# Attention stage of a fused layer stack: order of the second half's values, the output row and the key loads

## The chip, the cores and the metric

The kernel runs on one core of a Trainium2 chip. A core has five engines that run their own instruction streams and wait for each other by semaphores: TensorE (PE, matrix products; its weight loads are shown as PEld), VectorE (DVE), ScalarE (ACT), GpSimd (POOL) and SyncE (SP, here used only to start transfers). The metric is the device time of one launch in microseconds (us), lower being better. The kernel before is shown with three timed runs and one profiled execution.

## What is computed

A stack of six layers on a residual x of 4096 rows (2 sequences of 2048, read by the attention as 4 of 1024) by 256 columns: half a gated feed-forward, gated delta attention, half a feed-forward, half a binary-weight layer, a state-space convolution, half a binary-weight layer. The change lies in the attention. Its core, per head (16 heads of 16 columns) and chunk of 64 rows:

```
P = where(strict, (k_beta @ k.T) * L, 0)        # L = exp(g_i - g_j), lower triangle
Ainv = (I + P)(I + P^2)(I + P^4)...             # the inverse of a triangular matrix
v = Ainv @ v;  k_cumdecay = Ainv @ (k_beta * exp(g))
def step(S, inp):                               # scan over the chunks
    attn  = where(tril, (q @ k.T) * L, 0)
    v_new = v - k_cumdecay @ S
    o     = (q * exp(g)) @ S + attn @ v_new
    S     = S * exp(g_last) + (k * exp(g_last - g)).T @ v_new
o = o * rsqrt(mean(o*o) + 1e-5) * norm_w * silu(gate)
x = x + o @ Wo
```

## The kernel before, in words

The stages run one after another with a barrier between them (`phase_end`): first feed-forward, gates (which computes the decays and writes the normalized, turned x to a scratch in DRAM), delta (the attention), feed-forward, binary, space, binary. The delta stage works on 32 tiles of 128 rows (each in two halves of chunk length 64) with a software pipeline: `SLOTS` = 40 slots, and in slot n each engine runs a fixed list of steps, written out by hand, for tiles of different ages. `at(step, t)` runs a step for tile t if there is such a tile. LAG_FORM is 1, LAG_PAD 5, LAG_APPLY 6, LAG_SCAN 7 (the tile Z = n - 7 whose state is advanced) and LAG_OUT 8 (the tile O = n - 8 whose output row is finished).

PE, in slot n: values and states of the first half (`from_values` L1431, `from_state` L1450), `project_qk` (L1360) of tile n, `to_state` (L1463), the turned q and k and the decays of tile n - 1 (L1390, L1378, L1381), the second half's values and states, `project_vg` (L1370), `to_state` of the second half, `turn_o` (L1495) of O, `apply` (L1416, the product with the inverse T), `outputs` (L1481, L1486) of Z, `within` (L1400) of n - 1 and `project_o` (L1501) of O. The gate of tile n and `outputs` of tile Z are tied by a wait: `outputs` waits for the semaphore p_gate of tile n.

ACT: the copies y of the values (`keep_y`, L1615, halves 0 and 1), `widen` (L1631), the squares of q and k (L1530), `keep_kq` (the copies MV L1574 and KT L1575, the latter releasing the semaphore f_kt), `root_qk`, `exp_decays`, the value and gate copies and the sigmoid (L1557 to L1559), copies of the transposed output, WT, UT, the pad, and of the output (`keep_o`); `root_o` (L1549, L1550) is the reciprocal root of the output's mean square.

DVE interleaves two kinds of work: the triangular solve of a pair of tiles, in 58 steps of mostly one instruction each (L1750 to L1764; 29 in a slot, the first half in slots with even n), and small ones: `own_heads` (L1771, L1779), `new_state`, `sum_qk`, `faded_q` (QgT, L1704, which waits for f_kt), `keep_gate` (L1688), `scale_qk` (QK, L1696), `keep_within` and `keep_attn` (PT, AT, L1713), `sum_o` (L1790), `scale_o` (L1795), `add_o` (L1799).

POOL: the state's fades and sum (L1871, L1878, L1883), `gate_o` (L1887), `decayed_k` (L1854) and `kept_k` (L1864), which need QK. SP: all transfers of the stage, in the order of its slots: the turned x of tile n + 1, the decays, the keys out to DRAM (tile n - 1) and in again in another layout (`keys_in`, L1305, four transfers, tile n - 2), PT out and, by pairs of tiles, the matrices of the solve in and out. All transfers wait in SP's single order.

Of the kernel before, what the change touches and what calls it, by code (L numbers as in the profile page):

```python
# [12 lines left out]
P = 128  # L13
# [56 lines left out]
def build(nc, io):  # L70
    ctx = ExitStack()
    with ctx:
# [94 lines left out]
        late.close()  # L167
        B.gates_xn, B.ffn_xn, B.binary_xn = made["gates"].xn, made["ffn"].xn, made["binary"].xn
# [801 lines left out]
def gates_sync(e, B, M, S, run):  # L970
# [295 lines left out]

def delta_sync(e, B, M, S, run):
    Pd, Td = B.P_dram, B.T_dram

    def turned_in(t):  # L1270
        if t >= 2:
            e.wait_ge(S.p_vg, t - 1)
        b = t // BLK
        e.wait_ge(S.xt_out[b % 2], 32 * (b // 2 + 1))
        src = bass.AP(tensor=B.xT_dram, offset=t * P, ap=[[NT * P, P], [P * NT * P, KD], [1, P]])
        e.dma_start(M.xT[t % 2].rearrange("p (k n) -> p k n", k=KD), src).then_inc(S.p_in[t % 2], 16)
# [17 lines left out]

    def keys_in(t):

        e.wait_ge(S.k_out[t % 2], 16 * (t // 2 + 1))
        if t >= 2:
            e.wait_ge(S.k_in[t % 2], 64 * (t // 2))
        if t >= 7:  # L1300
            e.wait_ge(S.s_b, 2 * (t - 6))
        for r in range(4):
            src = bass.AP(tensor=B.Kd_dram, offset=t * P * DM + 8192 * r, ap=[[SUB, SUB], [1024, 8], [1, SUB]])
            dst = M.Kd[t % 7][SUB * r:SUB * r + SUB, :].rearrange("p (n c) -> p n c", n=8)
            e.dma_start(dst, src).then_inc(S.k_in[t % 2], 16)  # L1305
# [217 lines left out]
def delta_scalar(a, own, B, M, S, run):  # L1523
# [126 lines left out]
    for n in range(SLOTS):  # L1650
        Z = n - LAG_SCAN
        at(keep_y, Z, 0)
        at(root_o, n - LAG_OUT)
        at(widen, Z, 0)
        at(squares, n)
        at(keep_kq, n - LAG_FORM)
        at(root_qk, n)
        at(exp_decays, n - LAG_FORM)
        at(keep_y, Z, 1)
# [7 lines left out]
        at(keep_o, Z)  # L1667
    a.wait_ge(S.f_rstd, NBLK + 1)
# [5 lines left out]
def delta_vector(v, own, B, M, S, run):  # L1674
# [130 lines left out]
    for n in range(SLOTS):  # L1805
        Z, O = n - LAG_SCAN, n - LAG_OUT
        at(scale_o, O)
# [20 lines left out]
        solve(n, 24, 26)  # L1828
# [5 lines left out]
        at(sum_o, Z)  # L1834


def delta_gpsimd(g, own, B, M, S, run):
# [28 lines left out]

    def fade_first(t):
# [21 lines left out]
    for n in range(SLOTS):  # L1889
        Z, O = n - LAG_SCAN, n - LAG_OUT  # L1890
# [282 lines left out]
```

## Time and profile before

| | |
|---|---|
| runs shown | 1250.27, 1255.26, 1258.14 us (median 1255.26) |
| profiled execution | 1255.64 us, span 1253.8 us |
| granted PE clock, mean | 0.93 |
| PE / DVE / ACT / POOL busy | 1038.9 / 911.5 / 595.3 / 405.2 us |
| instructions | 38504 |
| delta stage | 224 to 844 us of the span |

A line of a timeline gives the start in us, the time that the instruction or group took, the engine, the line of the kernel, the operation with output and inputs, the number of instructions, and in brackets how long the engine had been idle ahead of it and which engine's work ended that. In a window the numbers behind the engines are busy us, in parentheses the instructions; behind them the granted clock of PE (1.00 is full speed), the share of the transfer engines and GB/s. The stage ends when x is complete, and the next one begins behind a barrier, so what the stage saves or loses the kernel saves or loses.

### The profile page before, as it was taken

How to read it: one execution, taken by the hardware profiler on the slowest of the kernel's cores; microseconds unless marked ns; L12 is line 12 of the kernel's file. 1: busy time of each engine (PE TensorE's matmuls, PEld its weight loads, DVE VectorE, ACT ScalarE, POOL GpSimd, SP SyncE). 2: the span in 40 equal slices, each digit the busy share in tenths (PEclk: the TensorE clock that was granted, in tenths of full speed). 3: DMA queues.
4: the chain of work that ended last, by engine and by line, in shares of the span. 5: the costliest groups of instructions: out<-in, count | busy, mean ns of one | idle time of the engine just before them, and what ended most of it. 6: DMA issues, size and time to landing. Idle time of an engine off the chain costs nothing. (4 is left out here: it accounts for less than half of the span.)

```text
span 1253.8 us, 38504 instructions
## 1 busy us (share of the span) xinstructions
PE 1038.9 (83%) x15542; PEld 738.8 (59%) x15542; DVE 911.5 (73%) x2403; ACT 595.3 (47%) x1614; POOL 405.2 (32%) x580
## 2 busy tenths in 40 slices
PE   2999977676888888888888876669999798799978
PEld 2888854344555555555555554548888664255556
DVE  3877646268888888988888888527776435899953
ACT  2433245344676666766767764454333352201152
POOL 2666530311221212122212221115665347500055
PEclk9999988798989999999999987779999889899979
DMA  9000012254444444444444443100000023944012
GB/s 259 8 2 1 1 56 101 61 103 95 105 96 95 92 91 91 105 101 96 83 97 99 100 93 75 36 3 1 1 1 1 17 57 79 268 135 135 1 34 101
DMA packets 282624, 93.30 MB, mean 74 GB/s; under 512 B 208976, under 2 KB 275408, under 8 KB 282448
## 3 DMA queue, kind: packets, MB, share of 16 engines
q1 hardware_dynamic: 280848, 88.23, 30.0%
q10 hardware_dynamic: 1600, 2.62, 0.7%
q8 instruction: 123, 2.02, 0.7%
q14 instruction: 53, 0.43, 0.1%
HBM read 56.20 MB, written 30.41 MB: 69 GB/s over the span
## 5 line engine op out<-in xcount | busy, mean ns | idle before, releaser
L1764 DVE TENSOR_TENSOR delta_tmp<-delta_PR 128x130 f32<-128x130 f32 (+12 forms) x416 | 156.5, 376 | 9.1
L1761 DVE TENSOR_TENSOR delta_PR<-delta_PR,delta_tmp 128x130 f32<-128x130 f32 (+12 forms) x416 | 152.7, 367 | 9.4
L1615 ACT ACTIVATE delta_y<-psum 32x128 f32<-32x128 f32 x256 | 68.1, 266 | 82.9 <-PE psum L1450 80.7
L1854 POOL TENSOR_TENSOR delta_VK<-delta_QK,both_eg 128x256 f32<-128x256 f32 x32 | 20.9, 653 | 253.7 <-DVE delta_QK L1696 253.7
L1416 PE MATMUL psum<-delta_T,delta_pad 128*32 128x128 f32 x2048 | 81.5, 326 | 17.5 <-DMA delta_T<-inverse_scratch 17.4
L1416 PEld LDWEIGHTS psum<-delta_T,delta_pad 128*32 128x32 f32 x2048 | 69.5, 133 | 28.3 <-DMA delta_T<-inverse_scratch 22.4
L1360 PE MATMUL psum<-both_w_in,delta_xT 128*128 128x512 f32 x128 | 68.0, 656 | 20.2 <-DMA delta_xT<-turned_scratch 10.2
L1878 POOL TENSOR_TENSOR delta_S<-delta_E,delta_Bm 128x128 f32<-128x128 f32 x32 | 16.4, 514 | 205.2 <-issue 198.2
L1463 PEld LDWEIGHTS psum<-delta_y,delta_Kd 32*32 32x32 f32 x2048 | 23.3, 112 | 99.3 <-ACT delta_y L1615 99.3
L506 POOL TENSOR_TENSOR ffn_H<-ffn_hid,ffn_H 128x512 fp32r<-128x512 f32 x48 | 61.7, 1290 | 57.2 <-DVE ffn_H L472 57.2
L1631 ACT ACTIVATE delta_wide<-delta_S 32x128 f32<-32x128 f32 x256 | 78.1, 305 | 3.1
L506 POOL TENSOR_TENSOR first_H<-first_hid,first_H 128x512 fp32r<-128x512 f32 x48 | 61.6, 1289 | 53.7 <-DVE first_H L472 53.7
L1463 PE MATMUL psum<-delta_y,delta_Kd 32*32 32x32 f32 x2048 | 30.6, 199 | 56.9 <-ACT delta_y L1615 56.9
L438 ACT ACTIVATE first_silu<-psum 128x512 f32<-128x512 f32 x48 | 28.7, 598 | 83.9 <-PE psum L391 83.9
L640 PE MATMUL psum<-w_bin,binary_XT 128*128 128x256 f32 x256 | 66.9, 407 | 0.0
L438 ACT ACTIVATE ffn_silu<-psum 128x512 f32<-128x512 f32 x48 | 28.7, 599 | 79.9 <-PE psum L391 79.9
L1370 PE MATMUL psum<-both_w_in,delta_xT 128*128 128x512 f32 x128 | 66.5, 645 | 0.0
L1400 PE MATMUL psum<-delta_MV,delta_KT 32*32 32x128 f32 x2048 | 63.9, 273 | 3.1 <-ACT delta_E L1565 3.1
L311 DVE BATCH_NORM_STATS2 ln_stats<-X 128x6 f32<-128x256 f32 x128 | 54.0, 422 | 16.6 <-DMA X<-in_x 14.4
L1400 PEld LDWEIGHTS psum<-delta_MV,delta_KT 32*32 32x32 f32 x2048 | 55.0, 107 | 12.8 <-issue 6.3
L709 DVE TENSOR_SCALAR binary_Y<-psum 128x512 f32<-128x512 f32 x32 | 22.1, 692 | 53.7 <-PE psum L640 53.7
L391 PE MATMUL psum<-first_XT,w_gate 128*128 128x512 f32 x192 | 54.6, 407 | 3.6 <-DVE first_XT L460 3.6
(282 smaller groups left out, 2599.0 us busy)
## 6 DMA issues: line engine op xcount, KB each, us to landing
within_scratch<-delta_PT SPq DMA_DIRECT2D x128, 64.0 KB, 1.9
delta_PR<-within_scratch SPq DMA_DIRECT2D x16, 512.0 KB, 4.3
inverse_scratch<-delta_PR SPq DMA_DIRECT2D x16, 512.0 KB, 3.3
delta_T<-inverse_scratch SPq DMA_DIRECT2D x128, 64.0 KB, 2.8
space_T<-taps_scratch SPq DMA_DIRECT2D x8, 1024.0 KB, 5.8
X<-taps_scratch SPq DMA_DIRECT2D x8, 1024.0 KB, 8.9
X<-in_x SPq DMA_DIRECT2D x32, 128.0 KB, 9.8
turned_scratch<-gates_XT SPq DMA_DIRECT2D x16, 256.0 KB, 2.3
```

The lines of the kernel that those rows point to most:

```text
L391: i = pe.matmul(bank[:], w[:, k * HID + m * P:k * HID + (m + 1) * P].bitcast(F32R), M.XT[b % 2][hl][k].bitcast(F32R), start=(k == 0 and hl ...
L438: a.activation(M.silu[n % 3], B.bank[n % 2][:], ACT.Silu, scale=1.0 / 127.0).then_inc(S.silu, 1)
L506: g.tensor_tensor(lo.bitcast(F32R), M.hid[n % 3], hi, ALU.subtract).then_inc(S.hid_lo, 1)
L640: i = pe.matmul(o[:, j * DM:(j + 1) * DM], M.XT[b % 3][k][:, (2 * h + j) * P:(2 * h + j + 1) * P], B.w_bin[:, k * DM:(k + 1) * DM], start= ...
L1360: i = pe.matmul(bank[4][:], M.xT[t % 2][:, k * P:(k + 1) * P], M.w_in[:, k, 0:512], start=(k == 0), stop=(k == 1))
L1370: i = pe.matmul(bank[5][:], M.xT[t % 2][:, k * P:(k + 1) * P], M.w_in[:, k, 512:1024], start=(k == 0), stop=(k == 1))
L1400: mm = pe.matmul(kk[g][rows, q * P:(q + 1) * P], M.KT[rows, g * P + SUB * q:g * P + SUB * q + SUB], M.MV[rows, (4 * g + q) * P:(4 * g + q ...
L1416: i = pe.matmul(bank[3][SUB * c:SUB * c + SUB, (2 * w + g) * P:(2 * w + g + 1) * P], M.pad[:, from_c:from_c + SUB], M.T[t % 2][:, h * P:(h ...
L1615: i = a.activation(dst, heads(bank[6][rows, half * P:(half + 1) * P]), ACT.Copy)
L1631: i = a.activation(states(M.wide[half])[rows, :, SUB * c:SUB * c + SUB], states(X)[rows, :, :], ACT.Copy)
L1761: i = v.tensor_tensor(after, after, t3, ALU.add)
L1764: i = v.tensor_tensor(t3, column.to_broadcast([P, j, n_after]), row.to_broadcast([P, j, n_after]), ALU.mult)
```

## The change

Five things. (1) The turned x of tiles 0 and 1 is loaded at the end of the gates stage (`turned_in` becomes a function that both stages call; the buffers xT of the delta stage are handed to the gates stage), instead of at the start of the delta stage. (2) On ACT the copy y of the second half's values stands ahead of the copies MV and KT. (3) The output row of a tile is finished in the slot of its scan: `sum_o`, `root_o`, `scale_o` and `gate_o` run in slot Z + 7 and no longer partly in the next. (4) On DVE QK stands ahead of the gate, and the gate four solve steps after `new_state` of the second half instead of three. (5) The loads `keys_in` are issued by POOL's queue, between the second fade and `decayed_k`, instead of SP's.

```diff
@@ gates_sync
+    for t in range(2):
+        turned_in(e, B, M.xT, S, t)
     taps_store(e, B, M, S)
@@ delta_sync
-    for n in range(-1, SLOTS):
-        at(turned_in, n + 1)
+    for n in range(SLOTS):
+        at(rows_in, n + 1)
         at(decays_in, n)
         at(keys_out, n - 1)
-        at(keys_in, n - 2)
@@ delta_scalar
         at(keep_y, Z, 0)
-        at(root_o, n - LAG_OUT)
         at(widen, Z, 0)
         at(squares, n)
+        at(keep_y, Z, 1)
         at(keep_kq, n - LAG_FORM)
         at(root_qk, n)
         at(exp_decays, n - LAG_FORM)
-        at(keep_y, Z, 1)
         at(widen, Z, 1)
...
         at(keep_o, Z)
+        at(root_o, Z)
@@ delta_vector
-        at(scale_o, O)
...
         at(new_state, Z, 1)
-        solve(n, 15, 18)
+        solve(n, 15, 16)
+        at(scale_qk, n)
+        solve(n, 16, 19)
         at(keep_gate, n)
-        solve(n, 18, 20)
-        at(scale_qk, n)
-        solve(n, 20, 23)
+        solve(n, 19, 22)
+        at(sum_o, Z)
+        solve(n, 22, 23)
         at(keep_within, n - LAG_FORM)
         solve(n, 23, 24)
         at(keep_attn, n - LAG_FORM)
-        solve(n, 24, 26)
+        solve(n, 24, 25)
+        at(scale_o, Z)
+        solve(n, 25, 26)
         at(add_o, O)
...
-        at(sum_o, Z)
@@ delta_gpsimd
+    def keys_in(t):
+        g.wait_ge(S.k_out[t % 2], 16 * (t // 2 + 1))
+        if t >= 2:
+            g.wait_ge(S.k_in[t % 2], 64 * (t // 2))
+        if t >= 7:
+            g.wait_ge(S.s_b, 2 * (t - 6))
+        for r in range(4):
+            ...
+            g.dma_start(dst, src).then_inc(S.k_in[t % 2], 16)
...
         at(fade_second, Z)
-        at(gate_o, O)
+        at(keys_in, n - 2)
         at(decayed_k, n)
         at(kept_k, n)
+        at(gate_o, Z)
```

On ACT, in a slot of the full stretch, the rows before, from the squares to the second `widen` (delta_y is the copy of the values, delta_KT the copy that f_kt announces):

```order
L1530 ACTIVATE delta_sq<-psum 128x512 [waits p_sum,p_qk]
L1574 ACTIVATE delta_MV<-psum,consts 128x2x8x32 [waits f_kk,f_kq_ps]
L1574 ACTIVATE delta_MV<-psum,consts 128x2x8x32
L1575 ACTIVATE delta_KT<-psum 128x256
L1542 ACTIVATE delta_rs<-delta_ssq,consts 128x32 [waits p_kn,p_sum]
L1543 ACTIVATE delta_rs<-delta_rs 128x32 [waits act_own]
L1565 ACTIVATE delta_E<-psum 128x512 [waits f_at,f_d]
L1615 ACTIVATE delta_y<-psum 32x8x16 [waits s_o,s_ws]
L1615 ACTIVATE delta_y<-psum 32x8x16 x3
L1631 ACTIVATE delta_wide<-delta_S 32x4x32 [waits s_o,s_1]
```

And now:

```order
L1525 ACTIVATE delta_sq<-psum 128x512 [waits p_sum,p_qk]
L1610 ACTIVATE delta_y<-psum 32x8x16 [waits s_o,s_ws]
L1610 ACTIVATE delta_y<-psum 32x8x16 x3
L1569 ACTIVATE delta_MV<-psum,consts 128x2x8x32 [waits f_kk,f_kq_ps]
L1569 ACTIVATE delta_MV<-psum,consts 128x2x8x32
L1570 ACTIVATE delta_KT<-psum 128x256
L1537 ACTIVATE delta_rs<-delta_ssq,consts 128x32 [waits p_kn,p_sum]
L1538 ACTIVATE delta_rs<-delta_rs 128x32 [waits act_own]
L1560 ACTIVATE delta_E<-psum 128x512 [waits f_at,f_d]
L1626 ACTIVATE delta_wide<-delta_S 32x4x32 [waits s_o,s_1]
```

The second half's delta_y has moved past MV, KT, the roots and the decays.

On DVE, the stretch from the state of the second half to PT (delta_tmp and delta_PR are the solve's), before:

```order
L1784 TENSOR_TENSOR delta_S<-delta_E,delta_Bm 128x128 [waits s_wide,s_e1,s_bm]
L1764 TENSOR_TENSOR delta_tmp<-delta_PR 128x198 [waits i_step]
L1761 TENSOR_TENSOR delta_PR<-delta_PR,delta_tmp 128x9x22 [waits i_step]
L1764 TENSOR_TENSOR delta_tmp<-delta_PR 128x210 [waits i_step]
L1688 TENSOR_TENSOR delta_gate<-delta_gate,psum 128x256 [waits p_sig,p_v]
L1761 TENSOR_TENSOR delta_PR<-delta_PR,delta_tmp 128x10x21 [waits i_step]
L1764 TENSOR_TENSOR delta_tmp<-delta_PR 128x220 [waits i_step]
L1696 TENSOR_TENSOR delta_QK<-psum,delta_rs 128x512 [waits p_kd,p_kg,f_kq_ps,p_rs]
L1761 TENSOR_TENSOR delta_PR<-delta_PR,delta_tmp 128x11x20 [waits i_step]
L1764 TENSOR_TENSOR delta_tmp<-delta_PR 128x228 [waits i_step]
L1761 TENSOR_TENSOR delta_PR<-delta_PR,delta_tmp 128x12x19 [waits i_step]
L1713 TENSOR_TENSOR delta_PT<-psum,delta_E 128x256 [waits i_out0,f_kk]
```

And now:

```order
L1779 TENSOR_TENSOR delta_S<-delta_E,delta_Bm 128x128 [waits s_wide,s_e1,s_bm]
L1759 TENSOR_TENSOR delta_tmp<-delta_PR 128x198 [waits i_step]
L1691 TENSOR_TENSOR delta_QK<-psum,delta_rs 128x512 [waits p_kd,p_kg,f_kq_ps,p_rs]
L1756 TENSOR_TENSOR delta_PR<-delta_PR,delta_tmp 128x9x22 [waits i_step]
L1759 TENSOR_TENSOR delta_tmp<-delta_PR 128x210 [waits i_step]
L1756 TENSOR_TENSOR delta_PR<-delta_PR,delta_tmp 128x10x21 [waits i_step]
L1683 TENSOR_TENSOR delta_gate<-delta_gate,psum 128x256 [waits p_sig,p_v]
L1759 TENSOR_TENSOR delta_tmp<-delta_PR 128x220 [waits i_step]
L1756 TENSOR_TENSOR delta_PR<-delta_PR,delta_tmp 128x11x20 [waits i_step]
L1759 TENSOR_TENSOR delta_tmp<-delta_PR 128x228 [waits i_step]
L1785 TENSOR_REDUCE delta_o_ss<-delta_o_sq 128x16 [waits o_rs,o_sq]
L1756 TENSOR_TENSOR delta_PR<-delta_PR,delta_tmp 128x12x19 [waits i_step]
L1708 TENSOR_TENSOR delta_PT<-psum,delta_E 128x256 [waits i_out0,f_kk]
```

QK has moved ahead of the gate and past four solve instructions, the gate is one solve instruction later, and `sum_o` (delta_o_ss) now stands ahead of PT.

On POOL, a slot, now (L1874 is `keys_in`; L1896 is `gate_o`, which stood behind the second fade before):

```order
L1880 TENSOR_TENSOR delta_E<-delta_S,both_egl 128x128 [waits s_x]
L1887 TENSOR_TENSOR delta_S<-delta_E,delta_Bm 128x128 [waits s_wide,s_bm,s_e0]
L1892 TENSOR_TENSOR delta_E<-delta_S,both_egl 128x128 [waits s_1]
L1874 DMA delta_Kd<-key_scratch 32x8x32 [waits s_b,k_in0,k_out0]
L1874 DMA delta_Kd<-key_scratch 32x8x32 x3
L1851 TENSOR_TENSOR delta_VK<-delta_QK,both_eg 128x16x16 [waits u_pad,p_kn]
L1861 TENSOR_TENSOR delta_Kd_tok<-delta_QK,both_bekd 128x4x32 [waits k_out0,p_kn]
L1861 TENSOR_TENSOR delta_Kd_tok<-delta_QK,both_bekd 128x4x32
L1896 TENSOR_TENSOR delta_o_sb<-delta_o_sb,delta_gate 128x256 [waits o_mul]
```

The four issues stand behind the second fade and ahead of `decayed_k` (delta_VK).

## Rows read from the trace of the kernel before

**Rows 1.** Windows of the whole core; engines' busy us (instructions), granted clock, DMA share.

```profile
308.20:740.40 432.20, 366.11 (x9735) 244.75 (x9727) 380.24 (x1136) 294.20 (x947) 93.70 (x174) 0.96 0.45 95
```

**Rows 2.** Windows of the twelve slots with even n; sum in the last line.

```profile
604.32:620.04 15.72, 14.02 (x391) 9.30 (x390) 13.90 (x46) 11.71 (x38) 3.81 (x7) 1.00 0.47 105
...
sum 196.36, PE 171.16 PEld 115.39 DVE 171.06 ACT 140.96 POOL 45.65; mean PE 14.26 PEld 9.62 DVE 14.25 ACT 11.75 POOL 3.80
```

**Rows 3.** Windows of the last five of these, 570.70 on: their sum.

```profile
sum 78.91, PE 69.71 PEld 46.59 DVE 69.50 ACT 58.67 POOL 19.07; mean PE 13.94 PEld 9.32 DVE 13.90 ACT 11.73 POOL 3.81
```

**Rows 4.** Windows: the slot n = 25, and two microseconds within it.

```profile
620.04:638.23 18.19, 15.52 (x390) 10.57 (x389) 16.00 (x46) 11.82 (x38) 3.76 (x7) 0.91 0.47 91
...
630.00:632.00 2.00, 1.78 (x50) 1.34 (x54) 1.86 (x7) 1.92 (x7) 0.00 (x0) 0.62 0.45 108
```

**Rows 5.** Timeline of PE, slots n = 24, 25: start, us, group, [idle before <-releaser].

```profile
609.21 0.48 PE L1450 MATMUL psum<-delta_X,delta_WT 32*32 32x32 f32 x32
...
616.08 0.65 PE L1481 MATMUL psum<-delta_y,delta_AT 128*32 128x64 f32 x32
...
630.22 0.52 PE L1463 MATMUL psum<-delta_y,delta_Kd 32*32 32x32 f32 x32 [2.00 <-ACT delta_y L1615]
...
631.28 3.20 PE L1416 MATMUL psum<-delta_T,delta_pad 128*32 128x128 f32 x64
634.31 0.62 PE L1481 MATMUL psum<-delta_y,delta_AT 128*32 128x64 f32 x32
```

**Rows 6.** Timeline of ACT, slots n = 24 and 25.

```profile
608.53 0.60 ACT L1530 ACTIVATE delta_sq<-psum 128x512 f32<-128x512 f32 x1
...
610.31 0.38 ACT L1575 ACTIVATE delta_KT<-psum 128x256 f32<-128x256 f32 x1
...
611.54 1.09 ACT L1615 ACTIVATE delta_y<-psum 32x128 f32<-32x128 f32 x4
...
615.08 0.42 ACT L1559 ACTIVATE delta_gate<-delta_gate 128x256 f32<-128x256 f32 x1
...
627.00 0.38 ACT L1575 ACTIVATE delta_KT<-psum 128x256 f32<-128x256 f32 x1
```

**Rows 7.** Timeline of DVE, slots n = 24 and 25.

```profile
607.39 0.43 DVE L1795 TENSOR_TENSOR delta_o_sb<-delta_o_sb,delta_o_rs 128x256 f32<-128x256 f32 x1 [0.62 <-ACT delta_o_rs L1550]
...
611.37 0.42 DVE L1704 TENSOR_TENSOR delta_QgT<-psum,delta_egT 128x256 f32<-128x256 f32 x1
...
615.60 0.42 DVE L1688 TENSOR_TENSOR delta_gate<-delta_gate,psum 128x256 f32<-128x256 f32 x1 [0.37 <-ACT delta_gate L1559]
...
626.67 0.81 DVE L1764 TENSOR_TENSOR delta_tmp<-delta_PR 128x234 f32<-128x234 f32 x1
...
629.59 0.42 DVE L1704 TENSOR_TENSOR delta_QgT<-psum,delta_egT 128x256 f32<-128x256 f32 x1
...
633.50 0.41 DVE L1688 TENSOR_TENSOR delta_gate<-delta_gate,psum 128x256 f32<-128x256 f32 x1
```

**Rows 8.** Timeline of POOL, slot n = 24.

```profile
617.41 0.69 POOL L1854 TENSOR_TENSOR delta_VK<-delta_QK,both_eg 128x256 f32<-128x256 f32 x1 [7.10 <-DVE delta_QK L1696]
```

**Rows 9.** Timelines of POOL, PE, ACT, DVE where the stage starts.

```profile
224.05 0.20 POOL L1839 MEMSET delta_S<- 128x128 f32 x1 [45.54 <-DVEq L171]
...
229.73 3.75 PE L1360 MATMUL psum<-both_w_in,delta_xT 128*128 128x512 f32 x4 [7.82 <-DMA delta_xT<-turned_scratch]
...
238.64 3.75 PE L1360 MATMUL psum<-both_w_in,delta_xT 128*128 128x512 f32 x4 [2.86 <-DVE delta_QK L1696]
...
235.28 0.23 ACT L1543 ACTIVATE delta_rs<-delta_rs 128x32 f32<-128x32 f32 x1
...
237.81 0.68 DVE L1696 TENSOR_TENSOR delta_QK<-psum,delta_rs 128x512 f32<-128x512 f32 x1
```

**Rows 10.** One line's DMA issues on SP: duration ns min/median/max.

```profile
L1305 SPq DMA_DIRECT2D delta_Kd<-key_scratch x128: 303/463/2098, 255.2 to 766.5; - x128
```

**Rows 11.** Timeline of PE, the stage's last slot.

```profile
840.91 0.44 PE L1495 MATMUL psum<-consts,delta_o_sb 128*128 128x128 f32 x2 [2.69 <-POOL delta_o_sb L1887]
```

More of the change, by code:

```diff
@@ L167, in build @@
         late.close()
+        made["gates"].xT = made["delta"].xT
         B.gates_xn, B.ffn_xn, B.binary_xn = made["gates"].xn, made["ffn"].xn, made["binary"].xn
@@ L1264, in at, with turned_in, rows_in @@
         stage(t, *more)
+def turned_in(e, B, xT, S, t):
+    b = t // BLK
+    e.wait_ge(S.xt_out[b % 2], 32 * (b // 2 + 1))
+    src = bass.AP(tensor=B.xT_dram, offset=t * P, ap=[[NT * P, P], [P * NT * P, KD], [1, P]])
+    e.dma_start(xT[t % 2].rearrange("p (k n) -> p k n", k=KD), src).then_inc(S.p_in[t % 2], 16)
 def delta_sync(e, B, M, S, run):
     Pd, Td = B.P_dram, B.T_dram
-    def turned_in(t):
+    def rows_in(t):
         if t >= 2:
             e.wait_ge(S.p_vg, t - 1)
[L1273 to L1276, printed above, removed]
+            turned_in(e, B, M.xT, S, t)
     def decays_in(t):
@@ L1293, in keys_out @@
         e.dma_start(dst, M.Kd_tok[t % 2].rearrange("p (n c) -> p n c", n=8)).then_inc(S.k_out[t % 2], 16)
[L1295 to L1305, printed above, removed]
     def pair_in(m):
@@ L1865, in kept_k @@
         i.then_inc(S.p_kd, 1)
+    def keys_in(t):
[5 more added lines that the diff above has]
+        for r in range(4):
+            src = bass.AP(tensor=B.Kd_dram, offset=t * P * DM + 8192 * r, ap=[[SUB, SUB], [1024, 8], [1, SUB]])
+            dst = M.Kd[t % 7][SUB * r:SUB * r + SUB, :].rearrange("p (n c) -> p n c", n=8)
+            g.dma_start(dst, src).then_inc(S.k_in[t % 2], 16)
     def fade_first(t):
@@ L1889, in delta_gpsimd @@
     for n in range(SLOTS):
-        Z, O = n - LAG_SCAN, n - LAG_OUT
+        Z = n - LAG_SCAN
         at(fade_first, Z)
```

## Prediction

> **What bounds the kernel now.** I read the windows first (what a full slot takes, and how busy each engine is), then the timelines of single slots (what the engine that ends last was waiting for), then those of the stage's two ends. The attention stage runs in 40 slots, and 25 of them, full ones, take 432.2 us of the span [rows 1], 17.29 us each. In them PE is busy 366 us and DVE 380; no engine is full, so the slot is a chain that goes from engine to engine. A slot with n even takes 16.36 us in the mean (twelve of them, 196.36) [rows 2], so one with n odd takes 235.8/13 = 18.1; the slot n = 25 is such a one, 18.19 [rows 4].
>
> The pair n = 24, 25 shows the chain. PE's slot n = 24 runs from 604.32 to 620.04 [rows 2]. DVE multiplies the gate at 615.60, and PE's `outputs` starts 0.48 us later, at 616.08; from there `outputs`, `within` and `project_o` run without a gap to the next slot at 620.04, 3.96 us [rows 5, 7]. So what ends last is the gate on DVE (`outputs` of one tile shares its turn with the gate of another), and a slot moves as the gate moves. In n = 24 the gate itself waited 0.37 us for the sigmoid on ACT, whose last step runs from 615.08 [rows 6, 7]: there two chains, DVE's and ACT's, end nearly together. In n = 25 DVE's gate stands at 633.50 without a wait, but the product with T ahead of `outputs` took 3.20 us at a granted clock of 0.62 (between the full 2.4 GHz and the lower level, 1.2), after PE had stood idle 2.00 us for the keys' half y [rows 4, 5]; `outputs` went at 634.31.
>
> **Part 1, the early rows.** Before, the stage opens at 224.05 (POOL's first instruction behind the barrier) and PE's first projection at 229.73, held by the load of the turned x [rows 9]. The load of tiles 0 and 1 now is issued in the stage before, behind the stores of the turned rows. The first projection can start right behind the barrier, at 224.1: 5.6 us. Then QK of tile 0: its scale was ready at 235.51, but it stood behind the gate and ran at 237.81, and PE waited 2.86 us for it [rows 9]. QK now goes ahead of the gate: 2.2 us. In slots 1 and 2 QK stands behind the gate too, and would give about 1 us each, as PE's own work there is next. The sum is 9.6 us (5.6 + 2.2 + 1.8) until the first triangular solve starts. It can't be over 12 (7.8 of wait at PE, 2.9 at QK, 1 more); it can be as little as 0 if the fill is bound by the loads of the decays, whose issues on SP stand where they stood. The nearest rows are those of PE, which waits for the rows and for QK and not for the decays, so I take 9.6.
>
> **Part 2, the slots with n even.** ACT now does the second half of y right behind the squares, ahead of the copies MV and KT. It needs `from_state` of the second half on PE, which starts at 609.21, behind PE's own row of work with no wait [rows 5]. `from_state` takes 0.48 [rows 5], so y can start at 609.73. ACT lost 0.6 us of work and a wait (root_o) ahead of the squares, which end at 609.13 now and at about 608.1 then [rows 6]. So ACT stands idle 1.6 us, y takes 1.09, MV 1.16, and KT starts at 612.0 instead of 610.31 and ends at 612.38. DVE's QgT waits for KT. It ran at 611.37, and DVE now comes to it 0.7 to 1.0 us earlier, since the wait of 0.62 for root_o is gone [rows 7]. So DVE stands 1.7 to 2.0 us and QgT runs at 612.40, 1.03 later than before. From QgT to the gate DVE had 4.23 us, of them 0.37 wait [rows 7]: 3.86. QK (0.68 by its row [rows 9], 0.60 net of its overlap with the next) and one more solve step (0.40, the length that a step has beside no POOL work) now lie ahead of the gate: 4.86. The gate stands at 617.26, 1.66 us later than 615.60, and the slot is 1.6 us longer. That holds for the last five even slots (78.9 us in all, 15.8 each) [rows 3]. The seven earlier ones take (196.36 - 78.9)/7 = 16.8, and the same chain gives about 17.3 there, +0.5. Sum: 5 x 1.6 + 7 x 0.5 = **+11.5**. Bounds: if QgT's wait didn't come, the gate would be bound by ACT, whose sigmoid chain is as long as before save for root_o, and the slot would be 16.3, no change (0). If every even slot paid 1.66, +19.9.
>
> **Part 3, the slots with n odd.** Here KT ended at 627.38 and DVE came to QgT at 629.59 [rows 6, 7], 2.2 us later; with y first KT ends at about 628.0, still half a microsecond or more ahead of DVE: no new wait. Gone are the wait of 0.62 and about 0.7 of sum_o and scale_o, which now run in the stretch behind the gate; QK and a step, 0.93, come ahead of the gate. The gate moves by -0.3 to 0 and the sum over 13 slots is -4 to 0. What PE gains at y (its 2.00 us of idle end earlier) turns into a wait for the gate, so I take **-0.6**.
>
> **Part 4, the tail.** In the last eight slots there is little solve left and the chain is root_o, scale_o, gate_o, turn_o, project_o. With sum_o, root_o, scale_o and gate_o done in the tile's own slot, the last row ends earlier: in the last slot PE waits 2.69 for gate_o on POOL [rows 11], and about 1.9 of that goes. Against it, in four slots in which the last solves run, scale_o and sum_o stand ahead of the result that is stored back: 0.35 + 1.3 + 1.0 (n = 32, 34, 35). I take **-0.2**, from -4 to +3.
>
> **Part 5, keys on GpSimd's queue.** SP issues 4 a tile at 0.46 us each, 2.1 at the most [rows 10], 1.9 us a slot that SP gets back; it only waits for PT with it: 0. On POOL they stand between the second fade (done about 5 us into the slot) and decayed_k, which waits 7.10 us for QK [rows 8]. POOL works 3.8 us a slot [rows 2]. By the rows four issues take 1.2 to 8.4 us; at 1.85 they fit in the 7.1, and only over 1.8 each would they be late. No row shows an issue from POOL. DVE's solve steps take 0.81 instead of 0.40 where a POOL instruction runs beside them (626.67) [rows 7]; if an issue did the same it would cost 0.4 a slot and issue. I take 0 and keep the rest as a rival.
>
> The Trainium skill, "SBUF — State Buffer", section "SBUF: two separate sides", speaks against this part: descriptors of a transfer that GpSimd's queue issues are written by GpSimd's cores, which are locked out of the port while DVE runs certain operations, and its next section gives about 620 ns alone and about 3100 ns beside a copy. By it, an estimate, four issues would take up to 12.4 us, and with POOL's own 3.8 the slot would be near its bound. No row of this trace shows such an issue.
>
> **The sum.** -9.6 + 11.5 - 0.6 - 0.2 + 0 = +1.1. To that comes PE's clock. PE will now stand idle ahead of `outputs` (for the gate) rather than ahead of y, 2 us and more, and in the slot n = 25 such a pause was followed by work at 0.62 [rows 4]. If it falls on `outputs` and `within` (3.2 us of work) and not on the product with T, it lies on the path; I put 1 to 2 us on it in the likeliest case. The profiled execution is 1255.64, by 0.4 above the median shown, so the forecast is 1255.6 + 2.4 = **1258**. Its own range is 1248 to 1268.
>
> **Rivals.**
> Faster, 0.24: QgT's wait stays hidden (y is not late in the even slots, or DVE's slack takes it up). Then part 2 is 0 and part 3 up to -4: 1255.6 - 9.6 - 2 = 1244. For it: ACT's and DVE's chains end within 0.4 us of each other [rows 7], and a shift of 0.5 us in either tips it. Against: the row of `from_state`, which has no wait to lose.
> Slower by the clock, 0.13: in the odd slots PE's pause ahead of `outputs` costs 0.9 to 2.1 us each, say 1.3 (3.2 us of work at 0.6 instead of 1.0 takes 2.1 longer, less the 3.20 x 0.38 = 1.2 that the product with T no longer loses, or all of it where that also stays slow). It decides once the pause is as long as the 2.00 of n = 25. Ten slots: 1258 + 13 = 1271.
> Slower by the issue on POOL, 0.18: from 1.8 us an issue, decayed_k and kept_k come late, with them the pad and the fades; or the issues slow DVE's solve steps, 4 x 0.4 = 1.6 us a slot, half of it on the path. At 0.6 to 0.8 us in 32 slots: +19 to +26, so 1277 to 1284. For it: 626.67. Against: the 7 us of room.
> The early load brings nothing (it queues behind the stores of the gates, or the decays bound the fill), 0.05: 1267.
> The forecast has 0.40.
>
> **How the numbers follow.** About 1% (12.5 us) is what a measurement of this kernel can tell from no change. Faster by it (below 1242.7) is about half of the first rival and the lower end of the forecast, with the tail: 0.20. Slower by it (above 1267.8): nearly all of clock and POOL, half of the lost load, the upper end of the forecast: 0.34. Within: 0.46. The range 1240 to 1278 leaves out a tenth at either end.
>
> **What would show it.** Right: PE's first projection at 224.1; on DVE a wait at QgT for KT of 1.7 us in the slots with n even alone, and even slots of 17.3; root_o's wait on DVE gone; odd slots within 0.3 of 18.1. Wrong: even slots of 16.3 or less; POOL's issues over 1.8 us or solve steps of 0.8 beside them; a granted clock under 0.7 at `outputs`. The sum fails most easily in part 2, as its +11.5 hangs on one wait.

## The result, and the profile after

The changed kernel takes 1277.42 us (median of 4, 1277.30 to 1284.25) where the kernel before took 1254.11 (4 runs): 1.0199 times as long, 95% interval 1.0152 to 1.0246. The forecast was 1258, 2.4 us more and no change that a measurement could tell; measured are 23.3 us more, clear of the interval. The time lies inside the stated range (1240 to 1278) by 0.6 us, but the size was missed. The profiled execution took 1284.25 us, 6.8 more than the median of the four, and spans 1282.5 us instead of 1253.8, so the differences by stage below are those of one execution each and add up to more than the 23.3 us. One of the ten runs of a later kernel, e7, took 1381.27 us at a granted clock of 0.73, a slower state, and is left out of its numbers.

Where the 28.7 us are, stage by stage, from the two traces: the first solve starts at 251.5 instead of 266.8 (-15.3, forecast -9.6); the 25 full slots take 467.2 instead of 432.2 (+35.0, forecast +10.9); the tail from there to the last product takes 110.2 instead of 102.6 (+7.6, forecast -0.2); the rest (+1.4) lies mostly in later stages. Of the start's 15.3 us, 1.6 are there because the stage before ended sooner (222.41 instead of 224.05).

The windows of the changed kernel, as [rows 1 and 2] had them; the last line of each group is the sum over its windows. First the 25 slots, then the twelve with n even, then the thirteen with n odd:

```profile
sum 467.18, PE 378.79 PEld 258.82 DVE 379.44 ACT 296.25 POOL 153.25; mean PE 378.79 PEld 258.82 DVE 379.44 ACT 296.25 POOL 153.25
```

```profile
sum 219.61, PE 180.67 PEld 124.53 DVE 173.07 ACT 142.47 POOL 72.91; mean PE 15.06 PEld 10.38 DVE 14.42 ACT 11.87 POOL 6.08
```

```profile
sum 247.57, PE 198.11 PEld 134.29 DVE 206.38 ACT 153.78 POOL 80.35; mean PE 15.24 PEld 10.33 DVE 15.88 ACT 11.83 POOL 6.18
```

DVE's work is the same (379 us); PE is 12.7 us busier with the same products, because it ran more of them at a low clock (granted clock 0.92 instead of 0.96 [rows 1]). Slots with n even went from 196.4 to 219.6, slots with n odd from 235.8 to 247.6.

What PE waited for in these 25 slots (engine and line, releaser: total, times, longest), in the kernel before and then in the changed one:

```profile
PE psum L1463 <- ACT delta_y L1615: 38.8, 25, 2.0
PE psum L1481 <- DVE delta_gate L1688: 10.5, 13, 1.0
PE psum L1431 <- DVE delta_Bm L1771: 6.8, 13, 0.8
PE psum L1416 <- DMA delta_T<-inverse_scratch: 5.3, 9, 1.1
PE psum L1450 <- DVE delta_X L1779: 4.2, 13, 0.3
```

```profile
PE psum L1411 <- DMA delta_T<-inverse_scratch: 59.4, 25, 4.2
PE psum L1476 <- DVE delta_gate L1683: 26.9, 15, 3.2
PE psum L1445 <- DVE delta_X L1774: 1.9, 6, 0.3
```

The wait for y is gone, and those for T and the gate grew from 15.8 to 86.3 us. PE's waits grew from 66 to 88 us, and they moved: from in front of `to_state` to in front of the product with T and of `outputs`. DVE's waits at sum_o and at QgT, 300 to 780 us:

```profile
DVE delta_o_ss L1785 <- ACT delta_o_sq L1633: 33.6, 26, 3.2
...
DVE delta_QgT L1699 <- ACT delta_KT L1570: 18.2, 13, 1.6
```

The slot n = 24 of the changed kernel, from 610.33, on DVE and on PE (start, us, group, idle before and its releaser):

```profile
618.45 0.42 DVE L1699 TENSOR_TENSOR delta_QgT<-psum,delta_egT 128x256 f32<-128x256 f32 x1 [1.60 <-ACT delta_KT L1570]
...
623.51 0.41 DVE L1683 TENSOR_TENSOR delta_gate<-delta_gate,psum 128x256 f32<-128x256 f32 x1
```

```profile
621.39 3.42 PE L1411 MATMUL psum<-delta_T,delta_pad 128*32 128x128 f32 x64 [3.02 <-DMA delta_T<-inverse_scratch]
624.57 0.88 PE L1476 MATMUL psum<-delta_y,delta_AT 128*32 128x64 f32 x32
```

The forecast wait at QgT is there, 1.60 us (forecast 1.7 to 2.0), and the gate stands at 13.18 us into the slot (forecast 12.94; 11.28 before [rows 7]). But `outputs` starts at 14.24 and not at 13.66, 0.48 behind the gate: PE had stood 3.02 us for T, and the product with T then took 3.42 us. That is the second thing. The forecast had half of it, the low clock behind a pause of PE, as a rival for the odd slots; that PE would stand for T stands nowhere in it.

The start, as [rows 9] (timelines of PE and DVE):

```profile
222.41 3.62 PE L1355 MATMUL psum<-both_w_in,delta_xT 128*128 128x512 f32 x4 [2.14 <-DVEq L172]
...
228.94 1.95 PE L1355 MATMUL psum<-both_w_in,delta_xT 128*128 128x512 f32 x4 [1.19 <-DVE delta_QK L1691]
```

```profile
251.52 0.09 DVE L1737 MEMSET delta_PR<- 128x32 f32 x1
```

PE waits for the stage's barrier and no longer for the load. The second projection ran 3.75 us at the low clock before and runs 1.95 now, so 1.8 of the extra 5.7 us of gain is clock. The pause right ahead of it shrank from 2.86 to 1.19 us, but it isn't that pause alone: in e5 below it is 3.04 us, and the projection takes 1.95 as well. What e5 and the changed kernel both lack is the 7.82 us of idle time ahead of the first projection.

The key loads on GpSimd's queue:

```profile
L1874 POOL DMA_DIRECT2D delta_Kd<-key_scratch x128: 582/582/798, 235.5 to 785.7; - x128
```

Each issue takes 0.58 us, 2.3 a slot, within the 7 us of room [rows 8]. The DVE steps beside them kept their length (0.26 to 0.29 us for the steps of 108 and 130 columns, as in the kernel before).

### The profile page after: what moved, and what is told of

The parts are those of the page before. It is cut to its first block and busy times, and to the rows that moved or that the text cites. A ratio compares the mean times of both kernels' runs of the same rounds, so it can differ in the third digit from the quotient of the medians.

```text
span 1282.5 us, 38504 instructions
## 1 busy us (share of the span) xinstructions
PE 1053.6 (82%) x15542; PEld 755.0 (59%) x15542; DVE 913.2 (71%) x2403; ACT 597.8 (47%) x1614; POOL 481.7 (38%) x708
## 5 line engine op out<-in xcount | busy, mean ns | idle before, releaser
L1759 DVE TENSOR_TENSOR delta_tmp<-delta_PR 128x130 f32<-128x130 f32 (+12 forms) x416 | 151.6, 364 | 8.6
L1411 PE MATMUL psum<-delta_T,delta_pad 128*32 128x128 f32 x2048 | 90.1, 349 | 76.8 <-DMA delta_T<-inverse_scratch 76.8
L1411 PEld LDWEIGHTS psum<-delta_T,delta_pad 128*32 128x32 f32 x2048 | 75.8, 141 | 88.7 <-DMA delta_T<-inverse_scratch 85.6
L1896 POOL TENSOR_TENSOR delta_o_sb<-delta_o_sb,delta_gate 128x256 f32<-128x256 f32 x32 | 24.6, 769 | 233.1 <-DVE delta_o_sb L1790 233.1
L1874 POOL DMA_DIRECT2D delta_Kd<-key_scratch x128 | 74.6, 590 | 9.0 <-DMA key_scratch<-delta_Kd_tok 5.6
L1395 PE MATMUL psum<-delta_MV,delta_KT 32*32 32x128 f32 x2048 | 71.6, 295 | 3.1 <-ACT delta_E L1560 3.1
L1355 PE MATMUL psum<-both_w_in,delta_xT 128*128 128x512 f32 x128 | 65.0, 631 | 6.7 <-DVE delta_QK L1691 3.0
L1395 PEld LDWEIGHTS psum<-delta_MV,delta_KT 32*32 32x32 f32 x2048 | 61.0, 116 | 14.7 <-ACT delta_E L1560 6.9
L439 ACT ACTIVATE first_silu<-psum 128x512 f32<-128x512 f32 x48 | 28.7, 599 | 83.2 <-PE psum L392 83.2
L439 ACT ACTIVATE ffn_silu<-psum 128x512 f32<-128x512 f32 x48 | 28.7, 599 | 81.1 <-PE psum L392 81.1
L1365 PE MATMUL psum<-both_w_in,delta_xT 128*128 128x512 f32 x128 | 64.1, 624 | 0.0
L641 PEld LDWEIGHTS psum<-w_bin,binary_XT 128*128 128x128 f32 x256 | 48.5, 200 | 14.3 <-issue 8.4
```

What stands on the lines that cost most here:

```text
L439: a.activation(M.silu[n % 3], B.bank[n % 2][:], ACT.Silu, scale=1.0 / 127.0).then_inc(S.silu, 1)
L641: i = pe.matmul(o[:, j * DM:(j + 1) * DM], M.XT[b % 3][k][:, (2 * h + j) * P:(2 * h + j + 1) * P], B.w_bin[:, k * DM:(k + 1) * DM], start= ...
L1355: i = pe.matmul(bank[4][:], M.xT[t % 2][:, k * P:(k + 1) * P], M.w_in[:, k, 0:512], start=(k == 0), stop=(k == 1))
L1365: i = pe.matmul(bank[5][:], M.xT[t % 2][:, k * P:(k + 1) * P], M.w_in[:, k, 512:1024], start=(k == 0), stop=(k == 1))
L1395: mm = pe.matmul(kk[g][rows, q * P:(q + 1) * P], M.KT[rows, g * P + SUB * q:g * P + SUB * q + SUB], M.MV[rows, (4 * g + q) * P:(4 * g + q ...
L1411: i = pe.matmul(bank[3][SUB * c:SUB * c + SUB, (2 * w + g) * P:(2 * w + g + 1) * P], M.pad[:, from_c:from_c + SUB], M.T[t % 2][:, h * P:(h ...
```

## Experiments

Most are the changed kernel or the one before with a single thing undone or done; e6, e7, e8, e11 and e12 combine more, as said there. The kernels ran on several chips, each beside runs of the kernel before on the same chip (medians of 1254 to 1258 us), so between kernels of different chips the ratios are the better comparison. Steady is the time of the same 25 full slots (432.2 before, 467.2 changed) in the one profiled execution; a wait's total is taken over 300 to 780 us, where the kernel before has 12.3 us for T and the changed kernel 63.2. A slot is called undisturbed if its granted clock is 1.00 and the gate, not the product with T, comes last ahead of `outputs`.

**Undo one at a time.** The first three kernels ran on the same chip as the fourth, e4.

e1_keys_sp:

```diff
 # delta_sync
         at(keys_out, n - 1)
+        at(keys_in, n - 2)
 # delta_gpsimd
-        at(keys_in, n - 2)
```

> The changed kernel with one thing undone: the key loads (keys_in) are issued by SyncE again, behind keys_out; all else stands as changed. Theory A (the key loads, issued by GpSimd at 5 us into the slot, run beside the loads of T, land them late, and PE's product with T waits 63 us for them): that wait falls to about 20 us, and the time falls by 15 to 25 us, to 1252 to 1262. Theory B (DVE stands in order at sum_o for ACT's copy of the output, 34 us in the changed kernel, so the solve and with it T are late, whoever loads the keys): the wait for T stays over 50 us and the time within 5 us of 1277. In both the waits of DVE at QgT (18 us) stay.

Measured: 1280.21 us, ratio 1.0182 (1.0128 to 1.0237). The time didn't change. Steady is 465.1, and PE's wait for T is still 54.6 us over 26 times. Theory A, which I had formed from the two traces, falls. Theory B is not refuted by it: DVE's wait at sum_o stays at 26.6.

e2_row_back:

```diff
 # delta_vector
+        at(scale_o, O)
         solve(n, 0, 1)
...
-        at(sum_o, Z)
...
-        at(scale_o, Z)
...
         solve(n, 27, 29)
+        at(sum_o, Z)
 # root_o and gate_o likewise in the slot behind
```

> The changed kernel with one thing undone: the output row as in the kernel before (sum_o at the end of DVE's slot, root_o, scale_o and gate_o in the next slot); keys still on GpSimd's queue, y ahead of the copies, QK ahead of the gate. Theory B: DVE's 34 us at sum_o go, the solve ends earlier, the wait for T falls well below 40 us and the time to about 1255 to 1262. Theory A: the wait for T stays at 50 to 65 us and the time between 1270 and 1280 (the wait of 0.6 us a slot for root_o comes back).

Measured: 1299.23 us, ratio 1.0317 (1.0295 to 1.0339), slower than the changed kernel by 15 us by the ratios (21.8 by the medians), and by 19 than e1 on the same chip. Theory B had its first half right and its second wrong: PE waits less for T (36.7 us), but the time rose. The odd slots take 269.9 us instead of 247.6: with root_o's wait back and QK ahead of the gate, the gate stands at 14.9 us into them instead of 13.7, PE idles 2.4 to 4.3 us ahead of `outputs` in twelve of them, and `within` behind it took over 2 us (1.95 at the full clock) in 11 of 13. So the output row in one slot is no cost there; it makes up for what QK ahead of the gate costs, as e12 below confirms from the other side. The tail is back at 102.5 us.

e3_y_back:

```diff
 # delta_scalar
         at(squares, n)
-        at(keep_y, Z, 1)
         at(keep_kq, n - LAG_FORM)
         at(root_qk, n)
         at(exp_decays, n - LAG_FORM)
+        at(keep_y, Z, 1)
```

> The changed kernel with one thing undone: on ScalarE the second half's y stands behind MV, KT, the roots and the decays again. The step of the prediction: the 13 waits of DVE at QgT (18 us) go. If the slot is bound by the gate behind QgT, the time falls by 8 to 15 us, to 1263 to 1269; if T's landing binds, as both theories A and B say, QgT's wait is hidden and the time changes by less than 4 us.

Measured: 1266.79 us, ratio 1.0072 (1.0038 to 1.0106): 10.6 us less than the changed kernel by the medians and 16 by the ratios, about as the step of the prediction had it. The waits at QgT are gone, the gate of the even slots is back at 11.7, and steady is 449.6. T's wait, still 35.5 us, keeps the even slots at 17.3 in the mean where undisturbed ones take 16.1.

e4_keys_only (the kernel before, `at(keys_in, n - 2)` moved from SP to GpSimd behind gate_o):

> The kernel before with one thing changed: the key loads are issued by GpSimd, behind the second fade and gate_o and ahead of decayed_k. Theory A: PE's wait for T rises from 17 us by 20 us or more and the time by 10 to 25 us, to 1265 to 1280. Theory B: no change, 1250 to 1258.

Measured: 1261.35 us, ratio 1.0011 (0.9981 to 1.0041): no change. (The median lies above the 1258 expected for that, but the kernel before was at 1258.06 on this chip.) Part 5's 0 holds when it is made alone.

**The start, and y with the keys.**

e5_early_rows (the kernel before with `turned_in` for tiles 0 and 1 in gates_sync):

> The kernel before with the early rows alone (turned x of tiles 0 and 1 loaded in the gates stage). The forecast of this part was 5.6 us of a start that came out 15.3 us shorter with QK ahead of the gate. Theory 'the start's parts add': 5 to 9 us faster than before. Rival: QK behind the gate holds PE in the fill anyway, and under 3 us are left.

Measured: 1251.80 us, ratio 0.9965 (0.9944 to 0.9987), 5.2 us less by the medians, 4.4 by the ratio. The first solve starts at 256.95, 9.8 us sooner; by the first full slot it is 8.1 (300.1 instead of 308.2).

e6_rows_fill_qk (e5, and in DVE's order):

```diff
+        if n < 7:
+            at(scale_qk, n)
         at(keep_gate, n)
         solve(n, 18, 20)
-        at(scale_qk, n)
+        if n >= 7:
+            at(scale_qk, n)
```

> The kernel before with the early rows, and QK ahead of the gate only in slots 0 to 6, where no solve lies between; full slots and the tail as before. If the changed kernel's loss lies in its full slots and its tail alone, this keeps the 15 us of the start and is 12 to 16 us faster than before (1240 to 1245). Rival: the first full slots are held by the loads of the decays or by SP, and the gain of the start is given back there: 1248 to 1255.

Measured: 1245.74 us, ratio 0.9921 (0.9896 to 0.9945): 11.3 us less than before by the medians. The solve starts at 253.2, steady is 432.5 and the tail 102.1, both as before. The time is just above the 1240 to 1245 that was expected. So the start's gain is real and its own, and nearly all that was lost was lost in the full slots and the tail.

e7_keys_y_back (e1 and e3 together):

> The changed kernel with two things undone: y behind the copies, and the key loads on SP. Undone alone, y gave 10.6 us and the keys nothing. If the key loads cost nothing (they only hid behind the late gate or not at all) it is as e3, 1264 to 1270; if they collide with the loads of T, which the late gate had hidden, it is 4 to 10 us faster than e3, 1257 to 1262.

Measured: 1262.61 us, ratio 1.0030 (1.0000 to 1.0059), 4.2 less than e3 on another chip, with runs that overlap (1253 to 1268, against 1260 to 1276), and between the two ranges that were expected. In the profiled executions the steady stretch is 9.0 us shorter (440.6 against 449.6). Once the gate no longer stands in front, the key loads beside T's may cost some us; the intervals of the two ratios overlap, and these runs can't tell.

**The clock.**

e8_t_twice (e1, and on PE):

```diff
     def apply(t):
...
-        for w in range(2):
+        for _ in range(2 if t % 2 and t < NT - 1 else 1):
+            for w in range(2):
```

> The kernel e1 (changed kernel, keys on SP) with PE's product with T done twice in the slots with n odd (same operands, the same result written twice), so that PE works 1.7 to 1.9 us longer in the time in which it waits for the gate. If PE's clock falls because of that idle time, `outputs`, `within` and `project_o` behind it run at the full clock in the odd slots, in which `within` took 3.2 us six times of twelve: these slots go from 19.1 to about 18.2 in the mean, and the time falls by 6 to 12 us, though work was added. If the clock falls for another reason, no such slot is mended, and the time stays or rises by up to 10 us.

Measured: 1282.44 us, ratio 1.0222 (1.0170 to 1.0275). The time didn't fall, against what was expected (e1 is at 1.0182, the intervals overlap); the slots tell why. In e1, `within` took over 2 us in 7 of the 13 odd slots and up to 3.6; in e8 in none. The odd slots take 241.7 us in all instead of 246.3, with the product done 13 times more in them. Where T was on time the second product filled the pause for nothing, where T was late (three slots, n = 9, 21, 27) both ran wholly or in part at the low clock, 5.0 to 6.5 us, and the tail grew by 9. So it is shown that work in the idle time takes the low clock off `within` (7 slots to none, in one execution each); the total that was expected of it isn't. What such a stretch looks like: the slot n = 29 in the changed kernel, windows around its `outputs` (length, busy us of the engines, then the granted clock) and the timeline of PE:

```profile
714.00:716.00 2.00, 1.13 (x24) 0.67 (x15) 1.93 (x6) 1.17 (x6) 1.52 (x3) 0.50 0.03 8
716.00:718.00 2.00, 1.90 (x52) 1.49 (x54) 0.86 (x4) 0.62 (x4) 0.00 (x0) 0.50 0.00 0
718.00:720.00 2.00, 2.00 (x44) 1.81 (x44) 0.60 (x2) 1.18 (x4) 0.00 (x0) 0.50 0.00 0
720.00:722.00 2.00, 2.00 (x36) 1.54 (x28) 0.72 (x3) 0.00 (x0) 0.00 (x0) 0.83 0.04 8
```

```profile
712.61 2.52 PE L1411 MATMUL psum<-delta_T,delta_pad 128*32 128x128 f32 x64 [2.30 <-DMA delta_T<-inverse_scratch]
716.10 1.08 PE L1476 MATMUL psum<-delta_y,delta_AT 128*32 128x64 f32 x32 [0.97 <-DVE delta_gate L1683]
716.95 1.08 PE L1481 MATMUL psum<-delta_wide,delta_QgT 128*32 128x128 f32 x16
717.96 3.24 PE L1395 MATMUL psum<-delta_MV,delta_KT 32*32 32x128 f32 x64
```

and the same slot in e8, with the product done twice:

```profile
709.50 3.70 PE L1425 MATMUL psum<-delta_T,delta_pad 128*32 128x128 f32 x128 [0.47 <-DMA delta_T<-inverse_scratch]
714.82 0.65 PE L1490 MATMUL psum<-delta_y,delta_AT 128*32 128x64 f32 x32 [1.62 <-DVE delta_gate L1697]
715.29 0.62 PE L1495 MATMUL psum<-delta_wide,delta_QgT 128*32 128x128 f32 x16
715.84 1.95 PE L1408 MATMUL psum<-delta_MV,delta_KT 32*32 32x128 f32 x64
```

The clock is at its lower level (0.50 of 2.4 GHz, 1.2) for 6 us and more behind two pauses of 2.30 and 0.97; `within` takes 3.24 instead of 1.95, and `outputs` 1.08 instead of 0.65. It is the low clock on this stretch, behind which nothing hides it, that makes a slot of 17.94 us (the same one in e1) into one of 20.07. The pair of slots is no proof by itself, as T was late by 2.30 us in one and by 0.47 in the other. And the length of a pause doesn't decide alone: in e1, without the second product, this slot kept the full clock through pauses of 1.43 and 2.40:

```profile
713.65 1.95 PE L1424 MATMUL psum<-delta_T,delta_pad 128*32 128x128 f32 x64 [1.43 <-DMA delta_T<-inverse_scratch]
718.01 0.65 PE L1489 MATMUL psum<-delta_y,delta_AT 128*32 128x64 f32 x32 [2.40 <-DVE delta_gate L1696]
718.48 0.62 PE L1494 MATMUL psum<-delta_wide,delta_QgT 128*32 128x128 f32 x16
719.03 1.95 PE L1408 MATMUL psum<-delta_MV,delta_KT 32*32 32x128 f32 x64
```

**The tail, and QgT.**

e9_factors_first:

```diff
-        at(gate_o, Z)
         if n in (SLOTS - 4, SLOTS - 3):
             first_factors(g, own, B, S, 1, n - (SLOTS - 4))
+        at(gate_o, Z)
```

> The changed kernel with the four small instructions of the next stage's row factors (1.9 us of GpSimd work, in slots n = 36 and 37) ahead of gate_o instead of behind it. If the tail's two late slots (13.95 us each where before had 12.0 and 11.1) come from the first fade that stands behind gate_o and these four in GpSimd's order, X of DVE no longer waits 1.5 us for it, and the tail of 110 us gets 3 to 4 us shorter, the whole time with it (1273 to 1275). If they come from T or the clock, the tail stays.

Measured: 1281.31 us, ratio 1.0201 (1.0170 to 1.0232), against 1.0199 for the changed kernel: the whole time didn't fall. In the profile the tail did, from 110.2 to 104.8 us, the slot n = 37 took 11.5 us instead of 14.0, and X waits 0.17 us at the most. The changed kernel's slot n = 37 on DVE and POOL:

```profile
845.48 0.29 DVE L1774 TENSOR_TENSOR delta_X<-delta_E,delta_Bm 128x128 f32<-128x128 f32 x1 [1.68 <-POOL delta_E L1880]
```

```profile
841.95 0.72 POOL L1896 TENSOR_TENSOR delta_o_sb<-delta_o_sb,delta_gate 128x256 f32<-128x256 f32 x1 [13.52 <-DVE delta_o_sb L1790]
842.75 0.24 POOL L304 TENSOR_SCALAR ln_shift<-ln_mean_var 128x4 f32<-128x4 f32 x1
...
843.37 1.04 POOL L306 TENSOR_TENSOR ln_rstd<-ln_rstd,minus_half 128x4 f32<-128x4 f32 x1
...
844.64 0.40 POOL L1880 TENSOR_TENSOR delta_E<-delta_S,both_egl 128x128 f32<-128x128 f32 x1
```

and e9's:

```profile
842.10 0.72 POOL L1896 TENSOR_TENSOR delta_o_sb<-delta_o_sb,delta_gate 128x256 f32<-128x256 f32 x1 [11.17 <-DVE delta_o_sb L1790]
842.79 0.40 POOL L1880 TENSOR_TENSOR delta_E<-delta_S,both_egl 128x128 f32<-128x128 f32 x1
```

So the place is shown (the first fade stood behind gate_o and 1.9 us of row factors); that it is worth 3 to 4 us of the time is not, and e1's tail was 106.9 us with that order as changed, so the tail itself varies by some us and not all of the 5.4 need be the order's.

e10_qgt_later:

```diff
-        at(faded_q, n - LAG_FORM)
-        solve(n, 9, 14)
+        solve(n, 9, 13)
+        at(faded_q, n - LAG_FORM)
+        solve(n, 13, 14)
```

> The changed kernel with QgT four solve steps later in DVE's order; y stays ahead of the copies. If DVE's wait for KT of 1.6 us at QgT is what moves the gate in the slots with n even (17.6 us undisturbed), the steps fill the wait, the gate moves from 13.2 back to about 11.9 and these slots to 16.3, and the time falls as in e3, by 8 to 16 us, to 1262 to 1270. If it is something else that y's new place does (PE reaching T sooner and idling), the time stays within 4 us of 1277.

Measured: 1268.43 us, ratio 1.0091 (1.0066 to 1.0116), 9 us less than the changed kernel by the medians and 14 by the ratios, with y where the change put it. The gate of the even slots is at 11.94 in the mean (expected 11.9) and the undisturbed ones take 16.31 (expected 16.3) instead of 17.60: QgT's wait is what they had lost. (The profiled execution is the slowest of the nine, 1275.36 us.) PE's wait for T is nearly unchanged at 61.7 us, and in seven of the twelve even slots `outputs` now starts as the late product with T ends, and they take 17.3 to 19.1.

**Versions that beat both.**

e11_best (e6, and in DVE's order):

```diff
+        at(sum_o, Z)
         solve(n, 27, 29)
-        at(sum_o, Z)
```

> The kernel e6 (before, early rows, QK ahead of the gate in slots 0 to 6) with sum_o two solve steps earlier in DVE's order, so that root_o is done on ScalarE while DVE steps on and scale_o finds it ready. The 25 waits of 0.62 us (15.6 us) go. In the slots with n odd the gate is bound by DVE's row of work, so 13 x 0.6 = 8 us come off; in those with n even the sigmoid on ScalarE binds 0.4 us behind, so 12 x 0.25 = 3. Expected 1234 to 1240. Rival: PE only comes to T sooner, waits for it and loses its clock, and nothing is left: 1243 to 1248.

Measured: 1241.72 us, ratio 0.9886 (0.9852 to 0.9919). The gate of the odd slots moved from 13.7 to 12.9, and steady from 432.5 to 425.7 (odd 234.7 to 229.0). That is 6.8 of the 11 expected, and the time lies between the two ranges. In most odd slots the product with T, at the low clock, now ends later than the gate, which fits the part that is missing.

e12_row_alone (e6, with the change's output row in one slot and e9's order on POOL):

> The kernel e6 (before, early rows, QK ahead of the gate in slots 0 to 6) with the change's output row in one slot (sum_o ahead of PT, root_o at the end of ScalarE's slot, scale_o behind AT, gate_o last on GpSimd but behind the next stage's row factors). It takes away the 0.62 us waits as e11 does, and puts about 1.3 us of DVE's work behind the gate, so the gate in the odd slots stands at about 12.4 and in the even ones at the sigmoid's 11.2. Theory 'the output row is the part of the change that pays': as e11 or better, 1234 to 1242. Rival: DVE stands in order at sum_o for ScalarE's copy (34 us in the changed kernel) and the solve, its store and T come 0.5 us later, which the earlier gate now uncovers: PE's wait for T rises from 17 to over 30 us, and the time is 1243 to 1252.

Measured: 1242.08 us, ratio 0.9904 (0.9868 to 0.9940). Both theories have their half. The gate stands at 12.45 in the odd slots and 10.66 in the even ones, and the odd slots take 221.0 us, 13.7 less than in e6, undisturbed ones 17.0 and 16.7. But PE's wait for T rose from 12.9 us in e6 to 35.2, and the even slots take 204.1, 6.2 more. With e2 this makes a square for the gate of the odd slots: 13.7 with neither the output row in one slot nor QK ahead of the gate (e6), 12.45 with the row alone (e12), 14.9 with QK alone (e2) and 13.7 with both (the changed kernel). So the row gives 1.2 us a slot and QK takes 1.2 back. The sums of the two kinds of slot, even and then odd:

```profile
sum 204.11, PE 175.09 PEld 119.93 DVE 171.84 ACT 143.55 POOL 44.22; mean PE 14.59 PEld 9.99 DVE 14.32 ACT 11.96 POOL 3.69
```

```profile
sum 220.96, PE 185.33 PEld 123.55 DVE 206.96 ACT 155.37 POOL 49.07; mean PE 14.26 PEld 9.50 DVE 15.92 ACT 11.95 POOL 3.77
```

e11 and e12 can't be told apart, and both are about 1% faster than the kernel before. Their intervals touch that of e6 (0.9896 to 0.9945), so what they add to it is read from the profiles more than from the times.

## Why the prediction was wrong, step by step

**Part 1, early rows and QK in the fill: right, too small.** Forecast -9.6 and at most -12, measured -15.3 in the trace. The rows alone brought the first solve 9.8 us forward where 5.6 were put down (e5), QK in the fill 3.7 more (e6). I had counted the wait and not that PE's first products had run at the low clock behind it (3.75 us for the second projection, 1.95 in e5), nor that the stage before ended 1.6 us sooner, at 222.4. That this part gave 5.7 us more than forecast is luck for the sum: it hides as much of what the other parts lost.

**Part 2, the even slots: right in mechanism, too small in size.** The wait at QgT (1.60) and the gate (13.2) came as worked out, and e3 and e10, two different ways to take the wait away, gave back 10.6 and 9.0 us by the medians (16 and 14 by the ratios). The undisturbed even slot takes 17.60 where I had 17.3 to 17.4. For the seven early slots I started from their mean of 16.8, which held slots that T or the clock had lengthened; the undisturbed ones took 16.24, so they lost 1.36 each and not 0.5. With 1.88 for each of the five late ones that makes 18.9 us for undisturbed slots alone, where the sum had 11.5; it is near the upper bound of 19.9 that the prediction gave.

**Part 3, the odd slots: right for an undisturbed one, wrong in the sum.** The gate stands at 13.67 in the mean in both kernels, and undisturbed slots take 18.26 us in the early part of the stretch and 17.93 in the late one (18.29 and 17.90 before). Forecast -0.6, measured +11.8.

**PE's waits and its clock, the step that failed.** The sum had 1 to 2 us for PE's clock, 13 in a rival with a chance of 0.13, and nothing for T. What lies over the undisturbed slots is 12 us more than before in the odd ones and 8.4 - 4.1 = 4 more in the even ones: 16 us. I had seen that PE's idle time would move to stand ahead of `outputs`, and had the row with the slow product behind such a pause; I priced it as if it would hit now and then. The prediction's own sign of being wrong, a granted clock under 0.7 at `outputs`, is there: 0.50 in the slot n = 29. e8 shows that work in PE's idle time keeps the full clock on `within`. And I had missed that PE stands for T too: 59.4 us in the full slots where it was 5.3. Two parts of the change do that. With y ahead PE gets through its second `to_state` sooner and comes to T sooner, where before the wait for y had covered T's landing; with y back (e3) the wait falls from 63.2 to 35.5 us. And with the output row in one slot DVE stands at sum_o with the solve behind it: with the row back (e2) the wait falls to 36.7, and the row alone (e12) raises it from 12.9 to 35.2. What is late next, behind a wait that is taken away, was named for the gate and not for T.

**Part 4, the tail: wrong.** Forecast -0.2, measured +7.6. In POOL's order gate_o now stands ahead of the next first fade, and in two slots the next stage's row factors with it; with the factors ahead (e9) the profile's tail is 5.4 us shorter. I had followed DVE's and ACT's queues there and not POOL's. The sum was off as well: its own terms, 1.9 gained and 0.35 + 1.3 + 1.0 lost, make +0.75 and not -0.2. The forecast also set the last row's gain at 1.9, and that one is there (PE waits 0.80 for gate_o instead of 2.69 [rows 11]).

**Part 5, the keys: right for the change made alone (e4) and in the changed kernel (e1).** The rival on POOL did not come: 0.58 us an issue, within the room. Its 1277 to 1284 us hold the measured time, but by accident. (By the prediction's rows four issues of 1.85 us make 7.4 and do not fit in the 7.1; at 0.58 it made no difference.) The Trainium skill ("SBUF — State Buffer", section "SBUF: two separate sides") warns that DVE, while it runs certain operations, keeps GpSimd from writing descriptors. No such stall shows in this trace: 128 issues took 582 ns in the median and 798 at the most, beside a DVE that was busy 81% of the stretch, and 2.3 us a slot were measured where the prediction's estimate, from a figure of that page's next section, was 12.4. Whether DVE's operations in this stretch are of the kind that the page means, no run here shows, so this is not a case against it.

What stays open: how much of the 16 us is T's lateness and how much the clock behind it, since they come together (a late T is a pause, and the product behind it is often slow); what, besides the length of a pause, decides whether the clock falls; and whether the key loads beside T's cost 0 or 4 us once the gate is early (e7).

## What to carry to other kernels

Before you take a wait away, look for what lands behind it unseen: here y's wait had covered the landing of T, and when it went PE waited for T, longer. Where the clock was seen to fall behind idle time, price a pause by what stands directly behind it on the path; idle time costs least where the slow work behind it is still hidden (here that is argued from the slots, as e8 gained no time by filling a pause). And when one step is moved on an in-order engine, follow every queue into the last slots too, where other work (here the next stage's factors) stands in the same row.

## What the runs showed of the hardware

PE's granted clock fell to 0.50 after pauses of 2.3 and 1.0 us in the slot n = 29 of the changed kernel and stayed there for some 6 us while PE was busy; in e8, with 1.75 us more of products ahead of `outputs`, it stayed up through pauses of 0.47 and 1.62, and in e1 through pauses of 1.43 and 2.40. So pauses of nearly the same length went both ways, and the low clock is paid not in the pause but in the 6 us behind it, 1.3 us on `within` alone. A transfer issue on GpSimd's queue took 0.58 us with hardly any spread, against 0.30 to 2.10 on SyncE's for the same transfers [rows 10], and landed after 2.4 us in the median instead of 2.1.
